# A cross-attention and mixture-of-experts block: the experts' rows routed in three parts, transposed and gated on the way, and gathered by adding

## The reference, cut to what matters

```python
# x: (64, 128, 128)   ctx: (64, 77, 96)   16 heads of 64
x = x + attention(layernorm(x), ctx, w_q, w_kv, w_out, b_out)
z = layernorm(x).reshape(8192, 128)
logits = z @ router_w.T                       # 8 experts, the best 2 of each row
gate[row, best two experts] = their logits
for e in range(8):                            # hidden size 176
    y = (silu(z @ w1[e].T) * (z @ w3[e].T)) @ w2[e].T
    moe_out += gate[:, e:e+1] * y
moe_out += (silu(z @ sw1.T) * (z @ sw3.T)) @ sw2.T     # shared expert, all rows
x = x + moe_out
```

## Time and profile before

| | us |
|---|---|
| median of 3 runs | 1151.36 (1148.72 to 1157.14) |
| the profiled execution | 1156.14 |
| its span, first to last instruction | 1153.5 |
| TensorE busy in the span | 954.7 |
| VectorE busy | 892.4 |
| GpSimd busy | 758.7 |
| ScalarE busy | 690.0 |
| mean granted TensorE clock | 0.923 of full |

### The profile page before, as it was taken

One profiled execution on the slowest core, in us unless ns is written; L12 is line 12 of the kernel. 1 busy time (PEld: TensorE's weight loads), 2 busy tenths in 40 slices (PEclk: granted clock), 3 DMA queues, 4 the chain that ended last, 5 costly groups with the idle time before them and its releaser, 6 DMA issues.

```text
span 1153.5 us, 29498 instructions
## 1 busy us (share of the span) xinstructions
PE 954.7 (83%) x10016; PEld 775.8 (67%) x10016; DVE 892.4 (77%) x2026; ACT 690.0 (60%) x1454; POOL 758.7 (66%) x1052
## 2 busy tenths in 40 slices
PE   5857899999999998999996999884868887676655
PEld 5555778887887777787884887664757775543333
DVE  4666689998988887898998897883666767786676
ACT  3544678777777766676774676662647764453222
POOL 2232567558778767777787577767765257787775
PEclk9878899999999999999998899996889999897776
DMA  8051233423444432332333443552444444452242
GB/s 261 4 153 30 42 53 74 128 53 72 68 66 72 70 61 56 70 74 59 75 72 61 81 70 62 78 130 50 130 128 141 128 125 129 115 143 78 79 137 73
DMA packets 209711, 102.39 MB, mean 89 GB/s; under 512 B 143488, under 2 KB 201504, under 8 KB 208576
## 3 DMA queue, kind: packets, MB, share of 16 engines
q1 hardware_dynamic: 201376, 83.72, 33.2%
q0 software_dynamic: 8192, 16.79, 5.2%
HBM read 39.65 MB, written 31.46 MB: 62 GB/s over the span
## 4 chain that ended last, share of the span: by engine, by line
PE 42%; issue 12%; POOL 12%; DVE 11%; DMA 10%; another core or an unknown queue 6%; ACT 4%; SPq 1%; DVEq 1%; POOLq 0%; ACTq 0%
DMA OT_lo<-O_lo 8%; PE Q L1219 5%; PE S L1153 5%; PE W L1093 4%; POOL O_lo L511 4%; PE W L1095 4%; PE W L1094 3%; PE W L1106 3%; PE W L1108 3%; PE W L1107 2%; DVE X L1059 2%; PE S L1206 2%; PE S L1207 2%; POOL rstd L456 1%
## 5 line engine op out<-in xcount | busy, mean ns | idle before, releaser
L961 DVE TENSOR_TENSOR pt_lo<-Q,pt_hi 77x512 f16<-77x512 f32 x256 | 164.5, 680 | 41.3 <-ACT pt_hi L622 40.5
L511 POOL TENSOR_TENSOR O_lo<-O,O_hi 128x512 f16<-128x512 f32 x128 | 146.5, 1164 | 33.6 <-ACT O_hi L630 18.5
L622 ACT ACTIVATE pt_hi<-Q 77x512 f16<-77x512 f32 x256 | 144.5, 590 | 27.2 <-PE Q L1219 25.8
L431 POOL DMA_INDIRECT xs<-x2cat,pos x128 | 134.8, 1053 | 31.1 <-issue 31.1
L538 POOL DMA_INDIRECT Yr<-ys,pos_y x128 | 125.9, 983 | 42.4 <-issue 32.0
L1219 PE MATMUL Q<-ident,P 128*77 128x128 f32 x1024 | 150.8, 281 | 1.7 <-ACT P L605 1.1
L1153 PE MATMUL S<-G,xTm 128*128 128x462 f32 (+1 forms) x384 | 145.3, 514 | 0.6 <-ACT G L612 0.6
L1206 PE MATMUL S<-v_hi,pt_hi 96*128 96x65 f16 x1024 | 109.3, 199 | 31.2 <-DVE P L930 28.8
L1219 PEld LDWEIGHTS Q<-ident,P 128*77 128x77 f32 x1024 | 124.6, 152 | 3.3 <-issue 1.7
L1206 PEld LDWEIGHTS S<-v_hi,pt_hi 96*128 96x128 f16 x1024 | 96.5, 99 | 41.5 <-DVE P L930 33.8
L1106 PE MATMUL W<-wo_hi,OT_hi 128*128 128x128 f16 x512 | 92.7, 224 | 36.9 <-DMA OT_lo<-O_lo 35.3
(11 more groups left out here) (211 smaller groups left out, 3287.9 us busy)
## 6 DMA issues: line engine op xcount, KB each, us to landing
xg<-xs SPq DMA_DIRECT2D x80, 128.0 KB
ys<-ysb SPq DMA_DIRECT2D x40, 256.0 KB
xp<-x2cat SPq DMA_DIRECT2D x64, 64.0 KB, 1.5
xg<-xp SPq DMA_DIRECT2D x16, 256.0 KB
y_out<-X SPq DMA_DIRECT2D x16, 256.0 KB
X<-x_in SPq DMA_DIRECT2D x1, 2304.0 KB, 10.2
xs<-x2cat,pos POOLq DMA_INDIRECT x128
xs<-zero_in SPq DMA_DIRECT2D x16, 128.0 KB, 2.5
```

The costliest lines, as they stand in the source:

```text
L431: pool.indirect_dma_start(out=xs_d[0 if b < PART[0] else 1][:, :], out_offset=index(pos, b, k), in_=x2cat[:, b % RING, :], in_offset=None) ...
L511: pool.tensor_tensor(O_lo[:, half_], O[:, (t + 1) % 2, half_], O_hi[:, half_], ALU.subtract).then_inc(s["p_Olo"], 1)
L622: act.activation(pt_hi[0:NK, j % 2, c * 512:(c + 1) * 512], QB[q_bank(j, c)][0:NK, :], ACT.Copy).then_inc(s["a_PThi"], 1)
L961: dve.tensor_tensor(pt_lo[0:NK, j % 2, c * 512:(c + 1) * 512], QB[q_bank(j, c)][0:NK, :], pt_hi[0:NK, j % 2, c * 512:(c + 1) * 512], ALU.s ...
```

## The change

The attention slots keep their order on TensorE. What changes:

- **Three parts** of 24, 24 and 16 batches instead of 40 and 24. Each part rounds up to whole items by itself, so there are 16 + 16 + 12 = 44 routed items, and 60 items instead of 56. The shared items come with the batches of the last part first (`ORDER`).
- **Transposed loads.** SyncE loads the rows of an item with DMA transposes straight into `xT` (four buffers). `rows_turn` on TensorE and `turned` on VectorE are gone.
- **Gates in the rows.** A row of `xs` has 264 instead of 256 two-byte elements, and the gate stands in the last ones. GpSimd writes it into `x2cat` before each scatter (`set_gate`), so that the two scatters of a batch now stand in neighbouring slots. SyncE loads the gates of an item with two small DMAs, and the results are multiplied with them when they are copied out of PSUM: by ScalarE in four instructions for even items, by VectorE in one for odd ones. The result bank alternates between two.
- **Gathers that add.** GpSimd's indirect DMA adds the gathered rows to `X` itself (`compute_op=ALU.add`). The ring `Yr` and VectorE's `mix` are gone. Gathers come four batches (eight DMAs) at a time at every other item: items 20 to 30 for the first part, 36 to 46 for the second, 48 to 54 for the third.
- **`low`** is done by GpSimd up to item 15 and by VectorE (`low_A`) from item 16 on.
- **Tables in six pieces**, one at the end of each of six slots, for each of the three parts.
- **The residual** of a batch is taken at the start of VectorE's next slot and not in the middle of the same one.
- Every engine does its item first and its late slot after it, where before the slot came first.

```diff
-PART = [40, 24]
+PART = [24, 24, 16]
+NP = len(PART)
...
+XC = 264
...
-        xs_d = [nc.dram_tensor(f"xs{p}", (XROWS, 2 * D), HF).ap() for p in range(2)]
+        xs_d = [nc.dram_tensor(f"xs{p}", (XROWS, XC), U16).ap() for p in range(NP)]
...
+        gathers = {}
+        b, n = 0, ROUTED[0] + LAG + 2
+        while b < NB:
+            ready = sum(PART[p] for p in range(NP) if first_of(p + 1) + LAG + 2 <= n)
+            take = [v for v in range(b, min(b + 4, ready))] if n % 2 == 0 else []
+            gathers[n] = take
...
             def load_rows(n):
                 if n >= XG:
-                    wait(sp, "f_T", n - XG + 1)
+                    wait(sp, "f_B", n - XG + 1)
...
-                        sp.dma_start(xg[:, n % XG, 2 * q:2 * q + 2, :],
-                                     xs_d[p][ds(v, GRAN), :].rearrange("(i p) n -> p i n", p=128)).then_inc(ring, 16)
+                        rows = xs_d[p][ds(v, GRAN), :]
+                        sp.dma_start(to[:, :, q * GRAN:(q + 1) * GRAN].bitcast(U16), rows[:, 0:2 * D], transpose=True).then_inc(ring, 16)
+                        sp.dma_start(gates[:, n % GR, 2 * q:2 * q + 2, :],
+                                     rows[:, 2 * D:2 * D + 2].rearrange("(i p) n -> p i n", p=128)).then_inc(s[f"gr{n % 4}"], 16)
...
+            def scatters(t):
+                one, two = t - S_SCATTER, t - S_SCATTER - 1
+                if on(two, 0, NB):
+                    set_gate(two, 1)
+                if on(one, 0, NB):
+                    set_gate(one, 0)
+                if on(two, 0, NB):
+                    pool.wait_ge(s["p_gate"], 2 * two + 2 + (two + 1 < NB))
+                    scatter(two, 1)
+                if on(one, 0, NB):
+                    pool.wait_ge(s["p_gate"], 2 * one + 1)
+                    scatter(one, 0)
...
-            def gather(b):
-                p = 0 if b < PART[0] else 1
-                wait(pool, "e_mix", 2 * (b - YR + 1))
-                for k in range(2):
-                    pool.indirect_dma_start(out=Yr[:, b % YR, k, :], out_offset=None, in_=ys_d[p][:, :],
-                                            in_offset=index(pos_y, b, k)).then_inc(s[f"ga{b % YR}"], 16)
+            def gather(b, k, n):
+                p = batch_part(b)
+                if k == 0:
+                    if n > shared_at(b):
+                        wait(pool, "e_X", ORDER.index(b // GB) + 1)
+                else:
+                    pool.wait_ge(s[f"ga{b % 8}"], 32 * (b // 8) + 16)
+                pool.indirect_dma_start(out=X[:, b, :], out_offset=None, in_=ys_d[p][:, :],
+                                        in_offset=index(pos_y, b, k), compute_op=ALU.add).then_inc(s[f"ga{b % 8}"], 16)
...
-                act.activation(ysb[:, m % 3, :], WB[2][:, :], ACT.Copy).then_inc(s["g_y"], 1)
+                act.wait_ge(s[f"gr{m % 4}"], 32 * (m // 4 + 1))
+                for i in range(GB):
+                    cols = slice(i * D, (i + 1) * D)
+                    last = act.activation(ysb[:, m % 3, cols], y_bank(m)[:, cols], ACT.Copy, scale=gates[:, m % GR, i, :].bitcast(F))
...
+                if on(t, 3, NB + 3):
+                    residual(t - 1)
                 if on(t, 0, NB):
                     piece_max(0); piece_max(1); piece_sub(0); piece_max(2); piece_sub(1); piece_sub(2)
...
                     pt_low(0); pt_low(1)
-                if on(t, 2, LAST):
-                    residual(t)
...
-                if t in TAB_SLOT:
-                    tables(TAB_SLOT.index(t))
+                for p in range(NP):
+                    if on(t - TAB_SLOT[p], 0, TAB_PIECES):
+                        tables(p, t - TAB_SLOT[p])
...
             for n in range(NI + LAG):
-                if any(turns(LAST + n)):
-                    turn(LAST + n)
-                if n + 1 < NI:
-                    rows_turn(n + 1)
                 if n < NI:
                     pcs[n] = pieces(n)
                     up_C(n, pcs[n])
                     up_A(n, pcs[n])
-                    if n == 0:
-                        project(LAST)
+                if any(turns(LAST + n)):
+                    turn(LAST + n)
+                if n == 0:
+                    project(LAST)
+                if n < NI:
                     up_B(n, pcs[n])
                 if n >= LAG:
                     down(n - LAG, pcs[n - LAG])
```

More of the change, by code:

```diff
@@ L249, in stored, with gathered, y_out, shared_at @@
         def stored(eng, b):
-            wait(eng, f"xp{b % RING}", 16 * (b // RING + 1))
-        def part_of(n):
-            return 0 if n < ROUTED[0] else 1
+            wait(eng, f"xp{b % 4}", 16 * (b // 4 + 1))
+        def gathered(eng, b):
+            wait(eng, f"ga{b % 8}", 32 * (b // 8 + 1))
+        def y_out(eng, m):
+            wait(eng, "g_y", m // 2 + 1)
+            wait(eng, "e_y", (m + 1) // 2)
+        def shared_at(b):
+            return NR + ORDER.index(b // GB) + LAG
+        def part_of(n):
+            return sum(n >= sum(ROUTED[:p + 1]) for p in range(NP - 1))
+        def first_of(p):
+            return sum(ROUTED[:p])
+        def batch_part(b):
+            return sum(b >= sum(PART[:p + 1]) for p in range(NP - 1))
+        def y_bank(m):
+            return (QB[0], WB[2])[m % 2]
+        gathers = {}
[4 more added lines that the diff above has]
+            gathers[n] = take
+            b += len(take)
+            n += 1
+        n_end = n
+        gather_at = {b: n for n, some in gathers.items() for b in some}
+        OUT_ORDER = sorted(range(NS), key=lambda i: max(NR + i + LAG, gather_at[ORDER[i] * GB + GB - 1]))
+        LOW_POOL = ROUTED[0]
         block = stack.enter_context(nc.Block())
@@ L723, in _ @@
                     gate_A(n)
+                if n > 0 and LAST + n <= TAIL:
+                    slot(LAST + n)
         @block.vector
@@ L1063, in _ @@
-            turned(0)
-            last_it = max(NI + LAG + 1, n_end + 2)
-            for n in range(last_it):
-                if LAST + n <= TAIL:
-                    slot(LAST + n)
-                if n + 1 < NI:
-                    turned(n + 1)
-                if n == 0:
-                    residual(LAST)
+            for n in range(NI + LAG + 2):
                 if on(n - 1, 0, NI):
                     low_C(n - 1)
+                if on(n - 1, LOW_POOL, NI):
+                    low_A(n - 1)
+                if on(n - LAG - 1, 0, NR) and (n - LAG - 1) % 2 == 1:
+                    result_out(n - LAG - 1)
+                if on(n - LAG - 1, NR, NI):
+                    shared_add(n - LAG - 1 - NR)
@@ L1076, in _ @@
                     hidden_A(n)
-                if on(n - LAG, NR, NI):
-                    shared_add(n - LAG - NR)
-                for b in gathers.get(n - 1, ()):
-                    mix(b, min(max(n - LAG - NR + 1, 0), NS))
+                if n > 0 and LAST + n <= TAIL:
+                    slot(LAST + n)
         @block.tensor
@@ L1281, in up_C @@
             def up_C(n, pieces_n):
-                wait(pe, "e_T", n + 1)
+                pe.wait_ge(s[f"xg{n % XG}"], sum(32 if m < NR else 16 for m in range(n % XG, n + 1, XG)))
                 if n == 0:
```

314 lines of the change are left out of this document (158 added, 156 removed).

## The result

The changed kernel is **slower**: 1237.39 us median (1235.73 to 1246.43, 4 runs) against 1151.57 (1148.72 to 1157.14) before, a ratio of 1.0755 (95% interval 1.0689 to 1.0821). The prediction was 1067 us. The profiled execution has a span of 1235.0 us, 81.5 more than before.

The account below looks back on a forecast made before the run. GpSimd was taken to bound the experts' second half. Terms 774 + 95 + 121 + 61 + 12 = 1063, GpSimd's chain 1062; 6 us for adding gathers made span 1069, time 1067 us, range 1025 to 1140.

Parts of the forecast that it names:

- Only because `hA_lo` is queued behind gathers: Second half of the experts' stage: GpSimd bounds it, as every item's down waits for four, later six, gathers.
- the other: GpSimd's own chain: second part's gathers from 955 us, 80 at 1.25 us, 7 us for the end, giving 1062.
- 12 pieces at 0.3 us, 4 us: Attention before item 0: table pieces fit VectorE's waits and cost 4 us (bounds 0 and 20), against 12 saved.
- sum -13 us for item 0: Attention up to item 0: -12 + 4 - 5, putting item 0 near 774 us.
- I take 5 us of the 52: Attention: gain from moving the residual, whose projection wait totals 51.9 us; bounds 0 and 30.
- The bound of +25: Attention up to item 0: upper bound on its change of -13 us; the lower was -35.
- 3.6 to 4.9 us; I take 4.4: Items 17 to 44: SyncE's time per item for store, table, gate loads and two transposes.
- Rival 3: Routed items: SyncE bounds at full transpose price, 5.2 us or more, time 1086; 6 or more, 1110; chance 0.12.
- I allow 0.05 to 0.1 us per adding gather: GpSimd's gathers: allowance for the addition, 6 us in all, making the span 1069.
- Rival 1: GpSimd: an adding gather costs more, step g; chance 0.13 for moderate g (1.4 to 2.06), 0.09 above.
- Its threshold of 2.06: GpSimd's gathers: step g in us from which the changed kernel is slower than before.
- Rival 2: Experts' stage: TensorE's late completions stay, some 6.4 us per item while GpSimd gathers, time 1110; chance 0.20.

Follow-up runs that it names:

- pieces_mid: Changed kernel with each table piece ahead of pt_low(2) instead of at the slot's end: 1199.48 us, ratio 1.0584, item 0 at 806.5.
- residual_mid: Changed kernel with VectorE's residual back in the middle of the slot, behind pt_low(1): 1216.58 us, ratio 1.071.
- mended: Changed kernel with tables as blocks, residual in mid-slot, and rows of items 0, 1, 2 loaded in slots 60, 62, 64: 1195.38 us, ratio 1.052.
- one_transpose: Changed kernel with one 512-row transposing DMA at a fixed place per routed item instead of two of 256 rows: 1193.94 us, ratio 1.0487.
- gates_off: Changed kernel without the gate loads, every gate 1: 1196.6 us, ratio 1.0547.
- gather_no_add: Changed kernel with gathers that overwrite X instead of adding to it: 1188.81 us, ratio 1.0424.
- before_low_dve: Kernel before with only hA_lo moved from GpSimd to VectorE from item 28 on: 1117.14 us, ratio 0.9817.

## Why the prediction was wrong

The diagnosis of the kernel before was right in the main: its second half was bound by GpSimd, and moving `hA_lo` alone gave 1.8%. "Only because `hA_lo` is queued behind gathers" was too much: with `hA_lo` moved, items 45 to 55 still took the 7.5 us of their six gathers. Then three costs of the change were set too low, and all three lie in one chain, the one that the prediction calls "the other": the start of the second part's gathers, 80 gathers, the end. It had 955 + 80 x 1.25 + 7; measured were 1076.6 + 80 x 1.86 + 10. Of the 166 us that the span is above the forecast of 1069, 122 are the late start (57 from item 0, 17 from items 0 to 17, 41 from items 17 to 36, and 7 that lie in the difference of the clocks and in the start of the gather), and 43 the gathers' price beyond the 6 us allowed for it.

1. **"12 pieces at 0.3 us, 4 us", sum -13 us for item 0.** Measured +43.6. A piece "fits where VectorE waits anyway" was argued from busy shares; the code puts it where VectorE does not wait. That place cost some 33 us (pieces_mid). "I take 5 us of the 52" for the residual: it was a loss (residual_mid 6.5 us at item 0 by itself, 13.7 in the time). Together with the early loads the three were 36 us: mended has item 0 back at 803. The bound of +25 was too low because it took a piece's length from the block, 1.7 us at most, where the twelve took 27.3, 2.3 each, and as much again went to the restart behind them. Nor does it follow from its own terms, -12 + 20 with the 24 of uncovered gate copies, which give +32; the measured value is beyond that too. The gate copies on GpSimd, feared as 24 us, were hidden as predicted: with the other causes gone the slots are those of before.
2. **SyncE, "3.6 to 4.9 us; I take 4.4".** 6.2 to 6.5. The upper price of a 256-row transpose (1.23) was the right one; the fixed part that the text mentions is all of it. With it the sum was 4.9; the 1.3 us that it did not hold are the gaps between five issues (0.19 + 0.17 + 0.19 + 0.44 in the rows above) and 0.3 more for the table, and single issues of up to 2.5 us make the mean 6.5. Rival 3 had this with 5.2 or "6 or more". Of the 17 us in items 0 to 17 some 8 are SyncE's too (one_transpose, gates_off); where the others come from was not tried.
3. **"I allow 0.05 to 0.1 us per adding gather".** 0.61: 1.86 us per step. Rival 1 has the right price range, but the end that it gives, 883 + 128 g + 7, is for a chain without a break, and that needs the forecast of the items: with items of 6.5 us the first part's 48 gathers end before the second's can begin even at 1.86. Its threshold of 2.06 is therefore void. With the second part's start at 1076.6 the end is near 1187 even at the old step of 1.25, and gather_no_add, which took the price away, was still slower than before by 4%. The rivals were priced one at a time on a base that itself was a forecast, and the case that came was all of them at once.

A small term besides: the 2.1 us that the prediction takes off its span came from one profiled execution that was slower than the median; the measured median is 2.4 above its span.

The sentence on the Trainium skill beside rival 1 (Collectives: The Full Stack, why ReduceScatter is half of AllGather) led to g near 1.9, and the measured 1.86 looks like it, but by luck: twice 0.94 is 1.88 for the instruction alone, and with the 0.30 behind it a step of 2.2. The instruction took 1.54, 1.6 times the plain one. Nor do the packets of GpSimd's queue double: 22528 in the changed kernel, 8192 in gather_no_add as before. The 128 gathers account for all 14336 more, 112 each on top of 32, so an adding one has 4.5 times the packets. Whether GpSimd's time goes with them is open, since leaving out the addition takes both away. The sentence that transpose DMAs are as fast as regular ones (Advanced Engine Details and Errata, X-Bar Transpose) is not borne out for the issuing side: 1.2 us against 0.4.

Rival 2 (late completions) fell: before_low_dve has none, so those waits went with `hA_lo` in GpSimd's queue. The shared items came out at 3.71 for 3.8.

## What to carry to other kernels

Work cut in pieces is free only in the very gap where the engine waits: read the timeline at the line where the piece will stand, and ask what is next behind it. A wait that ends on an engine with slack is not worth a place at the head of the slot. Before a transfer is split or made clever, count the issuing engine's instructions and multiply by the time of the nearest issue, not by its bytes. And where two chains end together in a forecast, compute the second from its own first instruction, with each uncertain term in it at its worst. Last, an average step hides a wait: divide by the number of steps only after the one long gap has been looked for.

## What the hardware showed

- **GpSimd and VectorE block each other.** At 487.25 us GpSimd starts two `O_lo` in the changed kernel; VectorE's L966 beside it, 256 elements in one partition, takes 1.27 us, until 488.68, when the first of them is just over:

```profile
487.25 2.45 POOL L567 TENSOR_TENSOR O_lo<-O,O_hi 128x512 f16<-128x512 f32 x2 [0.29 <-ACT O_hi L694]
```

  Sixteen operations in the twelve pieces before item 0 take 0.9 us or more in the changed kernel, L972 for 32 elements among them. Fourteen have two inputs in SBUF; the reductions are as long as in pieces_mid (0.2 to 0.55), and none of the same sixteen is long there, where the piece of this slot ends at 487.2 and `O_lo` begins at 487.8. The block before has it too: its L875 of 1.02 us in the earlier trace rows starts inside an `O_lo`. The Trainium skill (SBUF — State Buffer, Who interferes with whom) has the rule: the two engines share a port pair, which is "an exclusive lock". A VectorE instruction with two inputs in SBUF contends with a GpSimd one that reads SBUF, and in VectorE's two-port modes whoever issues first has the pair for the whole instruction. The traces agree; the overlap was not tried by itself.
- A transposing DMA costs its issuing engine 1.20 us for 256 rows and 1.24 to 1.26 for 512 (medians); a plain load or store 0.4.
- An indirect gather that adds holds GpSimd for 1.54 us, one that doesn't for 0.95, each with 0.30 behind it. Single ones of 1.5 and 2.0 us raise the step from one to the next to 1.34 and 1.86 (from the 49th to the last).
